# Delta-rule scan: two of the four transfers that spread the masked products are issued by ScalarE in place of SyncE

## The chip, the cores and the metric

The kernel runs on one core of one Trainium2 chip. The metric is the device time of one execution in microseconds (us). A core has five engines that each follow their own list of instructions: TensorE (PE), VectorE (DVE), ScalarE (ACT), GpSimd (POOL) and SyncE (SP). They meet only at semaphores. A transfer (DMA) is issued by an instruction in one engine's list and carried out by the core's 16 DMA engines; its landing adds 16 to a semaphore.

## What is computed

The program is a chain of seven further layers behind a first one; the change lies in the first, a delta-rule attention over 8 sequences of 512 tokens with 16 heads of 16 features. Its heart is a recurrence over the tokens:

```python
def step(M, inp):
    q_t, k_t, v_t, b_t = inp
    out_t = jnp.einsum('bnh,bnhd->bnd', q_t, M)
    retrieved = jnp.einsum('bnhd,bnd->bnh', M, k_t)
    delta = v_t - retrieved
    M = M + b_t[..., None, None] * jnp.einsum('bnh,bnd->bnhd', k_t, delta)
    return (M, out_t)
_, outs = jax.lax.scan(step, M0, xs)
```

The output rows are divided by their root mean square, multiplied by a weight, projected by Wo and added to x. Feed-forward, distance attention, a long convolution, mixtures and a state-space layer follow; the change does not touch them.

## The kernel before

The function `delta_scan` works in 32 chunks of 16 tokens. All 8 sequences and 16 heads of a chunk are treated at once, and one chunk needs the state matrix that the chunk before it left, so the chunks follow each other strictly. Each engine has a body `turn(ch, more)` that is written out for chunk after chunk; the order on an engine is the order in this code, and nothing reorders it. `ch.u` is 0 for the even chunks (0, 2, ...) and 1 for the odd ones: inputs are loaded for two chunks at a time, by the turns of odd chunks. `ch.j` is 0 in the first eight chunks; from the ninth on each turn also projects a finished tile of the output (`tile`, `tile_ready`, `root`, `tile_add`).

What one chunk does, with the lines that matter here:

- PE multiplies the keys with the state (psX, line 3471). DVE subtracts the result from the values (`wg`, L3739) and masks the products of queries and keys that PE formed in the chunk before (`qkm`, L3745, semaphore `qk_done`).
- PE forms the chunk's own key products (psB, L3486); DVE transposes them (`bg`, L3753, `bl_done`) and then solves a triangular system of 16 steps in `solve`: one copy (L3679), then by turns L3698, L3685 and L3692, all on DVE.
- The first reduction of the solve (L3692 with 26 outputs) reads columns of `pb` that ACT copies from `bg` (L3615, and L3617 for a later reduction): DVE waits for `pb_done` there.
- ACT's turn is, in this order: two scaled copies `wtm` (L3609), `take_out` (L3588: it reads what `within` left in PSUM and waits for `o_ps`), the two copies to `pb` (L3615, L3617, both behind `bl_done`), `tile_ready` (L3596, L3597), in odd chunks the load of `vT` (L3562), `keys` (L3579, L3582), `root` (L3602), four loads of `nbg` (L3571) and in odd chunks four loads of `qj` (L3567).
- The masked products lie in `qkm`, in four strips of 32 partitions. Four transfers from SBUF to SBUF, one for each strip, put them on the diagonal of `qkx` (L3386, 32 KB each). They wait for `qk_done` of this chunk and for `o_ps` of the chunk before, since `qkx` is a single buffer. PE reads `qkx` in `within` (L3439), which stands in its list behind the psB products of the next chunk and ahead of the products of L3505; L3505 also waits for `take_out`.
- SP's turn is in odd chunks: four loads of `kj` (L3344), eight of `kx` (L3353), the four `qkx` transfers, four loads of `nbx` (L3360). In even chunks: one load of `ng` (L3356), the four `qkx` transfers, four loads of `qx` (L3348).
- POOL folds the feed-forward weights beside the scan (`Butterfly.run`, L246 and L254), with a 1 MB load of `bf_w` (L228) every 24 us or so.
- `fill` (L3460) puts matmuls on PE whose results nobody reads.

Of the kernel before, what the change touches and what calls it, by code (L numbers as in the profile page):

```python
# [3244 lines left out]
def delta_scan(nc, core, tag, kx, feat, tok_nbk, wo, rms_w, masks, beside):  # L3245
# [17 lines left out]
    with ExitStack() as ctx:  # L3263
        sbf = lambda n, s: core.sbuf(f"{tag}_{n}", s, ctx)
        G, Q, H = 4, 32, 2
# [20 lines left out]
        qkm = sbf("qkm", [P, 2, G, G, CT])  # L3286
        qkx = sbf("qkx", [P, G, G, G, CT])
# [38 lines left out]
        strip = lambda n: slice(n * Q, (n + 1) * Q)  # L3326

        def chunks(eng, body):

            for n in range(CHUNKS):  # L3330
                body(Chunk(n // NCB, n % NCB // 2, n % 2), min(2, CHUNKS - 1 - n))
# [4 lines left out]
        @block.sync  # L3336
        def _(sp):

            flat = lambda rows: rows.rearrange("p j c g t -> p (j c g t)")

            def load_kj(c):
                src = k_d[c].rearrange("(i p) j n -> j p i n", i=G)
                for j in range(G):
                    sp.dma_start(kj[strip(j), j].rearrange("p i c g t -> p i (c g t)"), src[j]).then_inc(kj_in, 16)  # L3344

            def load_qx(c):
                for i in range(G):
                    sp.dma_start(flat(qx[strip(i), i]), q_d[c][strip(i)].rearrange("p j n -> p (j n)")).then_inc(qx_in, 16)  # L3348

            def load_kx(c):  # L3350
                for h in range(2 * G):
                    rows = slice(h * HD, (h + 1) * HD)
                    sp.dma_start(flat(kx[rows, h]), k_d[c][rows].rearrange("p j n -> p (j n)")).then_inc(kx_in, 16)  # L3353

            def load_ng(c):
                sp.dma_start(flat(ng[c % 2]), n_d[c].rearrange("p j n -> p (j n)")).then_inc(ng_in, 16)  # L3356

            def load_nbx(c):
                for j in range(G):
                    sp.dma_start(nbx[strip(j), j].rearrange("p (g f) -> p g f", g=G), nb_rows[c][j]).then_inc(nbx_in, 16)  # L3360

            load_ng(0)
            load_kx(0)
            sp.wait_ge(cleared, 1)
            load_qx(0)
            sp.wait_ge(zeroed, 1)
            load_nbx(0)
            sp.wait_ge(cleared, 2)
            load_kj(0)
            sp.dma_start(wo_sb[:], wo.rearrange("(k p) n -> p k n", p=P)).then_inc(loaded, 16)  # L3370
            sp.dma_start(rw[:], rms_w).then_inc(loaded, 16)

            def turn(ch, more):
                nxt = ch.pair(1)
                if ch.u and more:
                    ch.wait(sp, x_ps, 1, 1)
                    load_kj(nxt)
                    ch.wait(sp, b_ps, 1, 1)
                    load_kx(nxt)
                if ch.u == 0 and more == 2:  # L3380
                    ch.wait(sp, nbm_done, 2, 2)
                    load_ng(nxt)
                ch.wait(sp, qk_done, 1, 1)
                ch.wait(sp, o_ps, 1, 0)
                for g in range(G):
                    sp.dma_start(qkx[strip(g), g].rearrange("p j i t -> p (j i t)"),  # L3386
                                 qkm[strip(g), ch.n % 2].rearrange("p j i t -> p (j i t)")).then_inc(qkx_in, 16)
                if ch.u == 0 and more == 2:
                    ch.wait(sp, q_ps, 1, 2)
                    load_qx(nxt)  # L3390
                if ch.u and more:
                    ch.wait(sp, e_ps, 2, 2)
                    load_nbx(nxt)

            sp.wait_ge(zeroed, 3)
            chunks(sp, turn)
            sp.wait_ge(qkx_in, 64 * CHUNKS)

# [158 lines left out]
        @block.scalar  # L3557
        def _(act):
            a = nc.scalar.activation

            def load_v(c):
                act.dma_start(vT[:].rearrange("p j c g t -> p (j c g t)"), v_d[c].rearrange("p j n -> p (j n)")).then_inc(v_in, 16)  # L3562

            def load_qj(c):
                src = q_d[c].rearrange("(i p) j n -> j p i n", i=G)
                for j in range(G):
                    act.dma_start(qj[strip(j), j].rearrange("p i c g t -> p i (c g t)"), src[j]).then_inc(qj_in, 16)  # L3567

            def load_nbg(c):
                for g in range(G):  # L3570
                    act.dma_start(nbg[strip(g), c % 2, g].rearrange("p i f -> p (i f)"),  # L3571
                                  nb_cols[c][g].unsqueeze(0).broadcast_to([2, CT, 512])).then_inc(nbg_in[c % 2], 16)

            def keys(ch):

                split = lambda t: t.rearrange("p (j g) t -> p j g t", g=G)
                ch.pair_in(act, ng_in, 16)
                ch.wait(act, b_ps, 1, 0)
                a(split(wg[:, :, 1, :]), ng[ch.n // 2 % 2][:, :, ch.u], ACT.Identity).then_inc(wn_done, 1)  # L3579
                ch.wait(act, q_ps, 1, 0)  # L3580
                for e in range(2):
                    a(split(nbm[:, :, e, :]), ng[ch.n // 2 % 2][:, :, ch.u], ACT.Identity, scale=par[:, e:e + 1]).then_inc(nbm_done, 1)  # L3582

            def take_out(ch):

                pos = ch.cc * CT
                ch.wait(act, o_ps, 1, 1)
                a(oTb[:, ch.j % 2, :, pos:pos + CT], psO.rearrange("p j g t -> p (j g) t"),  # L3588
                  ACT.Identity).then_inc(oe_done, 1)

            def tile_ready(y, u, back):

                y.wait(act, y_ps, 1, -back)
                act.wait_ge(oe_done, NCB * (y.j + 1))
                src = oTb[:, y.j % 2, y.cc * KD:(y.cc + 1) * KD, :]
                a(oT[:, u], src, ACT.Identity).then_inc(oT_done, 1)  # L3596
                a(osq[:, u], src, ACT.Square).then_inc(osq_done, 1)  # L3597

            def root(y, u):

                y.wait(act, y_ps, 1, 1)
                a(r[:, u:u + 1], (psY, al)[u][:, D:D + 1], ACT.Sqrt, scale=1.0 / D, bias=eps6[:]).then_inc(root_done, 1)  # L3602

            def turn(ch, more):

                ch.wait(act, wt_done, 1, 1)
                ch.wait(act, w_ps, 1, 0)
                for e in range(2):
                    a(wtm[:, :, e, :], wg[:, :, 0, :], ACT.Identity, scale=par[:, e:e + 1]).then_inc(wtm_done, 1)  # L3609

                if ch.last():
                    take_out(ch.last())

                ch.wait(act, bl_done, 1, 1)
                a(window(pb, 7, [[8, 6], [48, 13]]), window(bg, 3 * Q + 2, [[1, 6], [Q, 13]]),  # L3615
                  ACT.Identity).then_inc(pb_done, 1)
                a(window(pb, 14 * 48 + 15, [[16, 8], [128, 7]]), window(bg, 9 * Q + 8, [[1, 8], [Q, 7]]),  # L3617
                  ACT.Identity).then_inc(pb_done, 1)

                if ch.j:  # L3620
                    tile_ready(Chunk(ch.j - 1, ch.pp, ch.u), 0, 0)

                if more:
                    if ch.u:
                        load_v(ch.pair(1))
                    keys(ch.next())

                if ch.j:
                    root(Chunk(ch.j - 1, ch.pp, ch.u), 0)
                if more:  # L3630
                    ch.wait(act, m_ps, 2, 0)
                    load_nbg(ch.n + 1)
                if more and ch.u:
                    ch.wait(act, o1_ps, 1, 1)
                    load_qj(ch.pair(1))

            load_v(0)
            act.dma_start(par[:], masks[0]).then_inc(masks_in, 16)
            act.dma_start(own[:].rearrange("p a t -> p (a t)"), masks[2]).then_inc(masks_in, 16)
            act.dma_start(causal[:], masks[1]).then_inc(masks_in, 16)  # L3640
            act.wait_ge(masks_in, 48)
            keys(Chunk(0, 0, 0))
            act.wait_ge(zeroed, 2)
            load_nbg(0)
            act.wait_ge(zeroed, 4)
            load_qj(0)
            act.wait_ge(eps_set, 1)
            chunks(act, turn)
            take_out(Chunk(TPB - 1, NCB // 2 - 1, 1))
            for n in range(NCB):  # L3650
                tile_ready(Chunk(TPB - 1, n // 2, n % 2), n % 2, min(n, 1))
                if n:
                    root(Chunk(TPB - 1, (n - 1) // 2, (n - 1) % 2), (n - 1) % 2)
            root(Chunk(TPB - 1, NCB // 2 - 1, 1), 1)
# [230 lines left out]
```

## Time and profile before

| | us |
|---|---|
| median of three runs | 2507.13 (2505.23 to 2515.93) |
| the profiled execution's own time | 2502.61 |
| its span, first to last instruction | 2500.8 |
| of this, the scan's chunks 1 to 31 | from 203.9 to 636.8 |

The profiled execution is one execution of the same program; its own time is a little below the three timed ones. In a timeline row the first number is the start from the beginning of the span, the second the time that the group took; "SPq" and "ACTq" are instructions of an engine's sequencer, here the issues of transfers. A number in square brackets is the time for which the engine was idle ahead of the row, and behind the arrow stands what ended it.

### The profile page before, as it was taken

Reading aid. Unit: us, or ns where it says so; the run is one execution under the profiler, and the core shown is the slowest. Engines: PE = TensorE matmul, PEld = TensorE weight load, DVE = VectorE, ACT = ScalarE, POOL = GpSimd, SP = SyncE. Lnnn points to the kernel's source line nnn. Section 1 sums busy time; section 2 is a strip of 40 time slices with the busy share of each in tenths; the row PEclk is TensorE's granted clock in tenths of the full one; section 3 lists DMA queues with packets and bytes.
Section 4 is the critical chain, followed back from the end, with each engine's and each line's share of the span. In section 5 each row is a group of like instructions: output and inputs, shape, how many; then the busy total and the mean of one; then the engine's idle time right before and its main releaser. Section 6 shows DMA issues by size and latency. Waiting matters only on the chain. (4 is left out here: it accounts for less than half of the span.)

```text
span 2500.8 us, 54327 instructions
## 1 busy us (share of the span) xinstructions
PE 2211.0 (88%) x21028; PEld 1618.1 (65%) x21028; DVE 1817.7 (73%) x4456; ACT 1406.0 (56%) x2163; POOL 1121.3 (45%) x1165
## 2 busy tenths in 40 slices
PE   7966767777899989999999988999898989999979
PEld 4535555555788845565656655998477856666669
DVE  6666778777766687888888865896664757767766
ACT  4531122222333279999999985655212567777755
POOL 4337999995001166677666852000351022233220
PEclk9989999999999989999999999999999999999999
DMA  5555444553100112112112211000001000000002
GB/s 175 152 156 163 128 147 138 166 156 102 63 1 14 41 55 69 56 61 69 57 54 74 67 44 38 1 1 1 15 1 40 1 1 1 1 1 1 1 1 68
DMA packets 158719, 148.87 MB, mean 60 GB/s; under 512 B 21440, under 2 KB 141376, under 8 KB 155392
## 3 DMA queue, kind: packets, MB, share of 16 engines
q1 hardware_dynamic: 138704, 105.51, 14.2%
q0 software_dynamic: 3456, 23.07, 2.8%
q10 hardware_dynamic: 16304, 16.83, 2.3%
q8 instruction: 168, 2.75, 0.5%
q14 instruction: 87, 0.71, 0.1%
HBM read 100.51 MB, written 40.63 MB: 56 GB/s over the span
## 5 line engine op out<-in xcount | busy, mean ns | idle before, releaser
L2057 DVE TENSOR_SCALAR_CACHE_REDUCE a_dist<-a_ring 128x512 f32<-128x512 f32 x512 | 336.5, 686 | 83.9 <-PE a_ring L1629 70.7
L2013 POOL TENSOR_SCALAR a_dist<-a_dist,a_mq 128x512 f32<-128x512 f32 x512 | 350.0, 712 | 66.6 <-ACT a_mq L1948 66.6
L1938 ACT ACTIVATE a_pT<-a_psT 128x1024 f32<-128x1024 f32 x256 | 257.9, 1025 | 56.4 <-PE a_psT L1641 40.1
L1641 PE MATMUL a_psT<-ident,a_dist 128*128 128x128 f32 x2048 | 272.2, 278 | 15.8 <-ACT a_pT L1938 12.6
L1641 PEld LDWEIGHTS a_psT<-ident,a_dist 128*128 128x128 f32 x2048 | 237.1, 143 | 56.7 <-issue 34.8
L1932 ACT ACTIVATE a_dist<-a_dist 128x2048 f32<-128x2048 f32 x128 | 236.0, 1901 | 14.5 <-DVE a_dist L2057 11.3
L3609 ACT ACTIVATE ds_wtm<-ds_wg,ds_par 128x256 f32<-128x256 f32 x64 | 29.1, 502 | 273.0 <-DVE ds_wg L3739 268.9
L1629 PE MATMUL a_ring<-a_stack 102*128 102x512 bf16 x512 | 175.5, 393 | 6.7 <-DVE a_dist L2057 5.1
L1258 POOL TENSOR_TENSOR c_y<-c_prod 128x1024 f32<-128x1024 f32 x16 | 39.2, 2472 | 294.5 <-DVE c_prod L1296 294.5
L1654 PE MATMUL a_psO<-a_pT,a_va 128*32 128x512 f32 x1024 | 133.7, 603 | 5.6 <-ACT a_pT L1938 5.6
L437 ACT ACTIVATE f_h<-a_psT,bf_bias_h 128x512 f32<-128x512 f32 x64 | 44.2, 690 | 125.9 <-PE a_psT L371 125.9
L2670 POOL TENSOR_TENSOR s_xdec<-s_xdt,s_dv 128x512 f32<-128x512 f32 x24 | 25.1, 1044 | 197.9 <-ACT s_dv L2596 188.1
L2696 DVE SCALAR_TENSOR_TENSOR s_xbc<-s_padded,sw_cw,s_xbc 128x512 f32<-128x512 f32 x144 | 107.5, 748 | 6.8 <-ACT s_xbc L2556 3.1
L1629 PEld LDWEIGHTS a_ring<-a_stack 102*128 102x128 bf16 x512 | 45.1, 98 | 101.9 <-DVE a_dist L2057 79.1
L2678 POOL TENSOR_TENSOR s_lt<-s_lt,s_gm 128x1024 f32<-128x1024 f32 x32 | 75.3, 2353 | 76.3 <-ACT s_lt L2606 76.3
L246 POOL TENSOR_TENSOR bf_t<-bf_up,bf_w 128x512 f32<-128x512 f32 x80 | 99.9, 1281 | 9.6 <-DMA bf_w<-in_up_w_dram 8.1
L246 POOL TENSOR_TENSOR bf_t<-bf_down_t,bf_w 128x512 f32<-128x512 f32 x80 | 100.3, 1288 | 1.6
L2405 PE MATMUL s_psP<-s_xnT,sw_win 128*128 128x512 f32 x192 | 91.5, 609 | 9.7 <-ACT s_xnT L2548 6.0
L1991 POOL TENSOR_TENSOR bf_up<-a_raw 128x512 f32<-128x512 f32 x28 | 32.8, 1173 | 145.6 <-DVE a_raw L2069 145.6
L480 DVE TENSOR_TENSOR f_h_lo<-f_h,f_h_hi 128x512 fp32r<-128x512 f32 x128 | 89.8, 702 | 4.4
L437 ACT ACTIVATE f_h<-f_psH,bf_bias_h 128x512 f32<-128x512 f32 x64 | 44.2, 690 | 70.1 <-PE f_psH L371 70.1
L478 DVE CAST f_h_hi<-f_h 128x512 fp32r<-128x512 f32 x128 | 56.1, 438 | 36.3 <-ACT f_h L437 36.1
(467 smaller groups left out, 6315.6 us busy)
## 6 DMA issues: line engine op xcount, KB each, us to landing
a_stack<-a_parts_dram SPq DMA_DIRECT2D x384, 64.0 KB
a_parts_dram<-a_parts SPq DMA_DIRECT2D x32, 384.0 KB, 2.4
bf_w<-in_up_w_dram POOLq DMA_DIRECT2D x10, 1024.0 KB, 5.6
bf_w<-in_down_w_dram POOLq DMA_DIRECT2D x10, 1024.0 KB, 7.7
ds_nbg<-tok_nbk ACTq DMA_DIRECT2D x128, 64.0 KB
feat_v<-di_part SPq DMA_DIRECT2D x16, 256.0 KB, 2.6
tok_nbk<-di_nbk SPq DMA_DIRECT2D x16, 256.0 KB, 2.9
feat_k<-di_part SPq DMA_DIRECT2D x16, 256.0 KB, 3.4
```

The lines of the kernel that those rows point to most:

```text
L246: e.tensor_tensor(t, v[:, :, i % 2, :], w, ALU.mult).then_inc(self.step, 1)
L437: gelu = lambda out: nc.scalar.activation(out, psH[m % 2], ACT.Gelu, bias=self.bf.bias_h[:, m:m + 1])
L480: tt(self.h_lo[:, m, :], self.h[:, n % self.RING, :], self.h_hi[:, m, :], ALU.subtract).then_inc(self.h_lo_done, 1)
L1629: mm(to[:], stack[0:NROW, u, 0, i, q * P:(q + 1) * P], stack[0:NROW, u, 1, i, :], start=True, stop=True).then_inc(ring_in, 1)
L1641: last = turn(psT[:, u % 2, kb, q * P:(q + 1) * P], dist[:, g % 2, i, q, k * P:(k + 1) * P], core.ident[:])
L1654: last = mm(psO[i * PAD:(i + 1) * PAD, :], va[:, par, kb, c:c + PAD], pT[:, i, kb // 2, kb % 2, :], start=(kb == 0), stop=(kb == TPB - 1))
L1932: a(dist[:, g % 2, i], dist[:, g % 2, i], ACT.Sqrt)
L1938: a(pT[:, u // 2, u % 2], psT[:, u % 2], ACT.Exp).then_inc(exp_done, 1)
L2013: last = nc.gpsimd.tensor_scalar(d, d, -1.0, mq[:, g % 2, i, q:q + 1], ALU.mult, ALU.add)
L2057: ts(dist[:, gg % 2, i, q, :], ps[:], 1e-12, 3.0e38, ALU.max, ALU.min, accum_out=mq[:, gg % 2, i, q:q + 1]).then_inc(ring_out, 1)
L2405: last = nc.tensor.matmul(out, lhsT, rhs, start=(k == 0), stop=(k == KD - 1))
L2696: last = stt(o, src[:, j:j + S], cw[:, c, j:j + 1], o, ALU.mult, ALU.add)
```

## The change

SP issues the transfers of strips 0 and 1 as before. Those of strips 2 and 3 are issued by ACT. In ACT's turn they stand behind `take_out` and ahead of the two copies to `pb`, with the same two waits. One wait for the memset of `qkx` is added on ACT ahead of the chunks; it stands behind a wait that already covers it.

```diff
@@ block.sync, turn @@
                 ch.wait(sp, qk_done, 1, 1)
                 ch.wait(sp, o_ps, 1, 0)
-                for g in range(G):
+                for g in range(G // 2):
                     sp.dma_start(qkx[strip(g), g].rearrange("p j i t -> p (j i t)"),
                                  qkm[strip(g), ch.n % 2].rearrange("p j i t -> p (j i t)")).then_inc(qkx_in, 16)
@@ block.scalar, turn @@
                 if ch.last():
                     take_out(ch.last())
 
+                ch.wait(act, qk_done, 1, 1)
+                ch.wait(act, o_ps, 1, 0)
+                for g in range(G // 2, G):
+                    act.dma_start(qkx[strip(g), g].rearrange("p j i t -> p (j i t)"),
+                                  qkm[strip(g), ch.n % 2].rearrange("p j i t -> p (j i t)")).then_inc(qkx_in, 16)
+
                 ch.wait(act, bl_done, 1, 1)
                 a(window(pb, 7, [[8, 6], [48, 13]]), window(bg, 3 * Q + 2, [[1, 6], [Q, 13]]),
                   ACT.Identity).then_inc(pb_done, 1)
@@ block.scalar, ahead of the chunks @@
             act.wait_ge(eps_set, 1)
+            act.wait_ge(zeroed, 3)
             chunks(act, turn)
```

ACT's list in the ninth chunk (the first with a tile), before:

```order
L3609 ACTIVATE ds_wtm<-ds_wg,ds_par 128x16x16 x2
L3588 ACTIVATE ds_oTb<-ds_psD0 128x16x16
L3615 ACTIVATE ds_pb<-ds_bg 128x6x13
L3617 ACTIVATE ds_pb<-ds_bg 128x8x7
L3596 ACTIVATE ds_oTq<-ds_oTb 128x256
L3597 ACTIVATE ds_oTq<-ds_oTb 128x256
```

The same place with the change (L3621 and L3623 are the copies to `pb` that were L3615 and L3617):

```order
L3609 ACTIVATE ds_wtm<-ds_wg,ds_par 128x16x16 x2
L3588 ACTIVATE ds_oTb<-ds_psD0 128x16x16
L3617 DMA ds_qkx<-ds_qkm 32x256 x2
L3621 ACTIVATE ds_pb<-ds_bg 128x6x13
L3623 ACTIVATE ds_pb<-ds_bg 128x8x7
L3596 ACTIVATE ds_oTq<-ds_oTb 128x256
L3597 ACTIVATE ds_oTq<-ds_oTb 128x256
```

Two issues of transfers now stand ahead of everything in ACT's turn but the `wtm` copies and `take_out`. SP's list differs only in the count of the `qkx` row, 2 in place of 4; the lists of PE, DVE and POOL are the same.

## Rows read from the trace of the kernel before

**Rows 1.** The page: busy time of each engine and its share

```profile
PE 2211.0 (88%) x21028; PEld 1618.1 (65%) x21028; DVE 1817.7 (73%) x4456; ACT 1406.0 (56%) x2163; POOL 1121.3 (45%) x1165
```

**Rows 2.** Stretches by window: length, busy of each engine, granted clock, DMA share, GB/s

```profile
core 0: us, PE busy (x) PEld busy (x) DVE busy (x) ACT busy (x) POOL busy (x), PEclk, DMA share, GB/s
203.85:636.80 432.95, 309.35 (x9316) 246.80 (x9316) 334.50 (x1034) 109.04 (x320) 384.16 (x317) 0.97 0.48 137
314.98:328.32 13.34, 9.58 (x302) 7.76 (x302) 10.95 (x35) 3.73 (x11) 12.87 (x11) 1.00 0.63 202
297.89:314.98 17.09, 11.83 (x302) 9.61 (x302) 10.96 (x34) 3.69 (x11) 16.78 (x15) 0.80 0.33 94
522.44:540.00 17.56, 12.25 (x302) 9.47 (x302) 11.04 (x34) 3.74 (x11) 17.00 (x15) 0.81 0.67 174
607.55:623.48 15.93, 12.67 (x302) 10.24 (x302) 11.02 (x35) 3.68 (x11) 0.00 (x0) 0.79 0.16 44
```

**Rows 3.** Last work of POOL's folding and of DVE's scan, by line

```profile
L254 POOL TENSOR_TENSOR bf_down_t<-bf_t x40: 1259/1278/1301, 445.0 to 598.8; 128x512 f32<-128x512 f32 x40
L3718 DVE BATCH_NORM_STATS2 bn<-X x32: 409/418/420, 312.7 to 649.2; 128x6 f32<-128x256 f32 x32
```

**Rows 4.** Timeline of an odd chunk without a late transfer

```profile
314.98 0.42 DVE L3739 TENSOR_TENSOR ds_wg<-ds_vT,ds_psXQ 128x256 f32<-128x256 f32 x1
...
317.05 0.38 ACT L3588 ACTIVATE ds_oTb<-ds_psD 128x256 f32<-128x256 f32 x1 [0.70 <-PE ds_psD L3439]
317.35 0.34 ACT L3615 ACTIVATE ds_pb<-ds_bg 128x78 f32<-128x78 f32 x1
...
318.13 0.24 DVE L3692 TENSOR_REDUCE ds_al<-ds_pb 128x26 f32<-128x78 f32 x1
```

**Rows 5.** Timeline of the next chunk, with a late transfer

```profile
330.74 0.65 PE L3439 MATMUL ds_psD<-ds_qkx,ds_dm 128*32 128x64 f32 x32 [0.87 <-DMA ds_qkx<-ds_qkm]
...
331.46 0.38 ACT L3588 ACTIVATE ds_oTb<-ds_psD 128x256 f32<-128x256 f32 x1 [1.78 <-PE ds_psD L3439]
331.50 1.16 SPq L3386 DMA_DIRECT2D ds_qkx<-ds_qkm  x2
331.74 0.33 ACT L3615 ACTIVATE ds_pb<-ds_bg 128x78 f32<-128x78 f32 x1
...
332.18 0.24 DVE L3692 TENSOR_REDUCE ds_al<-ds_pb 128x26 f32<-128x78 f32 x1 [0.74 <-ACT ds_pb L3615]
```

**Rows 6.** Chain of waits in the scan (184 to 640): us in total, times, longest

```profile
DVE ds_al L3692 <- ACT ds_pb L3615: 11.9, 8, 3.5
...
PE ds_psD L3439 <- DMA ds_qkx<-ds_qkm: 8.1, 6, 3.2
...
PE ds_psD L3439 <- issue: 4.4, 2, 2.2
```

**Rows 7.** Timeline, three of those eight waits of DVE

```profile
304.52 0.24 DVE L3692 TENSOR_REDUCE ds_al<-ds_pb 128x26 f32<-128x78 f32 x1 [3.52 <-ACT ds_pb L3615]
375.19 0.24 DVE L3692 TENSOR_REDUCE ds_al<-ds_pb 128x26 f32<-128x78 f32 x1 [2.02 <-ACT ds_pb L3615]
512.20 0.24 DVE L3692 TENSOR_REDUCE ds_al<-ds_pb 128x26 f32<-128x78 f32 x1 [2.09 <-ACT ds_pb L3615]
```

**Rows 8.** Timeline of SP over the odd chunk of rows 4

```profile
316.67 5.48 SPq L3353 DMA_DIRECT2D ds_kx<-feat_k  x8
322.25 3.47 SPq L3386 DMA_DIRECT2D ds_qkx<-ds_qkm  x4
325.77 3.66 SPq L3360 DMA_DIRECT2D ds_nbx<-tok_nbk  x4
```

**Rows 9.** Timeline of ACT at the scan's start

```profile
183.60 2.06 ACTq L3567 DMA_DIRECT2D ds_qj<-feat_q  x4
185.77 0.91 ACT L3609 ACTIVATE ds_wtm<-ds_wg,ds_par 128x256 f32<-128x256 f32 x2 [4.11 <-issue]
```

**Rows 10.** Issues by line: duration ns min/median/max, first and last start us

```profile
L3386 SPq DMA_DIRECT2D ds_qkx<-ds_qkm x128: 507/592/1689, 187.1 to 627.6; - x128
L3571 ACTq DMA_DIRECT2D ds_nbg<-tok_nbk x128: 597/599/1200, 180.5 to 617.6; - x128
L3562 ACTq DMA_DIRECT2D ds_vT<-feat_v x16: 338/339/381, 173.9 to 596.7; - x16
```

**Rows 11.** Timeline, four issues of nbg by ACT

```profile
334.61 2.51 ACTq L3571 DMA_DIRECT2D ds_nbg<-tok_nbk  x4
```

## The prediction

> **What bounds the kernel now.** The page comes first: PE is busy for 88% of the span, DVE for 73% [rows 1], but that mean covers stages with different limits, and the change lies in one of them. So I read the scan by windows. Its chunks 1 to 31 take 432.95 us, in which DVE is busy for 334.50, PE for 309.35 and ACT for 109.04 [rows 2]. No engine fills the stretch: each chunk is a chain that passes between PE and DVE, and DVE's solve is its longest piece. A chunk without trouble takes 13.34 us, with DVE busy for 10.95 [rows 2]. POOL looks full (384.16 us), but its folding ends 50 us ahead of the scan: its last group starts at 598.8, DVE's last at 649.2 [rows 3]. What lengthens DVE's chain lengthens the kernel, until it is many times what is discussed here.
>
> In the timeline of one clean chunk the reader is to see how close ACT's copy to pb comes to that chain. `take_out` starts at 317.05, the copy L3615 0.30 us behind it at 317.35, and it ends at 317.69. The reduction L3692 that needs it starts at 318.13 [rows 4]. In a chunk where it was late it ran from 331.74 to 332.07 and the reduction began at 332.18, 0.11 later [rows 5]. So in the clean chunk the copy could have been later by 318.13 - 317.69 - 0.11 = 0.33 us. More than that shifts the solve and everything behind it.
>
> Last the waits, for what the change can win. DVE waits for that copy 8 times, 11.9 us in all, and PE waits in `within` for the `qkx` transfers 6 times, 8.1 us [rows 6]. These are mostly the same events: transfers late, `within` late, `take_out` late, and the copy stands behind `take_out` ([rows 5] show one such chain). Two of the eight, 2.02 and 2.09 us [rows 7], go with the two waits of PE of 4.4 us that are put down to issue [rows 6], at which no transfer is named. That leaves 11.9 - 4.1 = 7.8 us that late `qkx` transfers cost. Why they are late: in an odd chunk SP issues eight `kx` loads first (5.48 us), then the four `qkx` transfers in 3.47 us up to 325.72 [rows 8], though nothing but the `kx` issues stood between it and them for those 5.48 us, and PE could not read them before 330.74 [rows 5].
>
> **The change, part by part.** Two issues leave SP. They were the last two of a group of four. SP's share starts when it did and ends a pair earlier; two take 1.16 us in [rows 5], half of 3.47, that is 1.74, in [rows 8]. ACT's pair now goes out right behind `take_out`, in odd chunks some 5 us before SP gets to its own.
>
> Two issues come to ACT. Does ACT stand still while it issues? [rows 9] say so: four `qj` issues run from 183.60 to 185.66, and the `wtm` copy behind them starts at 185.77, after 4.11 us of idle time that no engine caused. It was held by the issues and ran 0.11 us after the last. What does one issue cost there? No row shows `qkx` on ACT. The nearest are the same transfer on SP, 592 ns median, and ACT's `nbg` load, also to 32 partitions, 599 ns median [rows 10]. A pair takes 1.16 us on SP [rows 5] and half of 2.51, 1.25 us, on ACT [rows 11]. I take 1.20. The bounds: 0.34 us each as ACT's `vT` load, 339 ns [rows 10], which with a gap of 0.03 makes 0.71 for the pair; and 1.74 us, half of the 3.47 in [rows 8], where issues were stretched.
>
> Where does the pair begin? SP's first `qkx` issue follows 0.04 us behind the start of `take_out`, both released by the same semaphore [rows 5]; ACT's will too. So the copy to pb starts 0.04 + 1.20 + 0.11 = 1.35 us behind the start of `take_out`, where it was 0.30: it is 1.05 late. 0.33 is free, so the reduction and all that follows shift by 0.72 us. Over 32 chunks: 23.0 us. The first has no `take_out`, but the same two issues ahead of the copy; I count it in full.
>
> What this delay drags along: behind the copy in ACT's list stand the second copy, `tile_ready`, the `vT` load, `keys`, `root` and the loads of `nbg` and `qj`. The second copy is read three reductions further on, and PE waits for `tile_ready` and `keys` only late in the solve, which itself moves by 0.72: nothing. The waits on `qk_done` and `o_ps` on ACT add nothing, as `qkm` is written ahead of `bg` on DVE and `take_out` has waited for `o_ps` already. The wait on the memset is covered.
>
> What comes back: the reduction now waits in every chunk, and lateness of `within` adds on top. A transfer may be later by the SP pair saved (1.20) and by the stretch of the chunk between (0.72), 1.92 us in all, before it is seen. In terms of DVE's wait, a lateness is the wait plus the 0.33 that were free. The longest was 3.52 + 0.33 = 3.85; 1.93 of it remains. The other five are below 1.92 (7.8 - 3.52 = 4.3 us for five, 0.74 in [rows 5]) and vanish. The two waits without a transfer stay, and count 2.02 + 0.33 and 2.09 + 0.33, 4.77 together. Sum of DVE's waits there after the change: 23.0 + 1.9 + 4.8 = 29.7; before: 11.9. The difference is 17.8 us.
>
> The sum is made against the profiled execution's 2502.61: 2520.4. The median of the three runs is 4.5 us above that execution, so the same 17.8 on the median give **2525 us**.
>
> A rule speaks for less: the Trainium skill, page "DMA: Bandwidth & Descriptors", section "Issuing engines are not separate DMA queues", says that starting transfers from several engines saves only the sequencer's time, as all of them interleave on the same 16 engines. If that is all, nothing lands earlier by a less crowded queue; it would leave the late landings as they are. No row here decides it, and it stands behind the first rival.
>
> **The rivals.**
>
> 1. The late transfers stay late. For it: the chunks after them carry much traffic (the DMA share is 0.63 in the odd chunk before [rows 5] [rows 2]), and the last `qkx` issue ended 5 us before PE could go on, longer than the issues themselves. Against: SP's ring then holds two transfers fewer. The sum is 23.0 + 8 x 0.33 = 25.6 us more: 2533. This is what the rule above would make of it.
>
> 2. The issue on ACT is cheap or does not hold ACT: not slower. If each costs what `vT` costs (0.71 the pair), the copy is 0.04 + 0.71 + 0.11 - 0.30 = 0.56 late and DVE shifts by 0.23 a chunk, 7.4 us; the longest lateness keeps 3.85 - 1.20 - 0.23 = 2.4, with the 4.8 that is 7.2, and 7.4 + 7.2 - 11.9 is +2.7: 2510. If the copies went past the issues, no chunk would shift, the waits fall from 11.9 to 4.1 + (3.52 - 1.20) = 6.4, and the time is 2501.6. For it: ACT starts an issue while earlier activations still run. Against: what matters is an activation behind issues, and [rows 9] show that held. It decides where the pair holds ACT for less than 0.04 + x + 0.11 = 0.63, x = 0.48 us: below, no chunk is shifted.
>
> 3. Issues stretched as in [rows 8]: a pair of 1.74 makes 1.26 a chunk, 40.3 + 6.7 - 11.9 = +35: 2542. For it: in odd chunks SP issues `kx` at the same time. Against: ACT's `nbg` issues hold 597 to 599 ns in minimum and median [rows 10].
>
> 4. TensorE's clock. Three windows of a chunk have a granted clock of 0.80, 0.81 and 0.79, and took 17.09, 17.56 and 15.93 us where a chunk at 1.00 took 13.34 [rows 2]; the first had the 3.52 us wait, in which PE stood idle. The last had 1.09 of waiting and lost 1.5 more to the clock (15.93 - 13.34 - 1.09). The change puts 0.7 us of idle time on PE into each chunk, ahead of the tile. If in six more chunks the clock fell to the lower of its two levels (1.2 GHz of 2.4) for part of their time, at 2.6 us each (between 1.5 and 4.2), the time is 2541. Against: clean chunks with gaps keep 1.00.
>
> **How the numbers follow.** Forecast 55% (own range 2517 to 2531: a pair of 1.13 to 1.3, with more or less of the late landings gone); rival 1 12%; rival 2 cheap 8%, not held 8%; rival 3 7%; rival 4 10%. The predicted time is the forecast's, 2525. The range is 2508 to 2541: below it lies the case where ACT is not held and a tail of the cheap one, above it half of rivals 3 and 4. 0.5% is 12.5 us, about what a measurement of this kernel can tell from no change; slower by more begins at 2519.7. That takes in rivals 1, 3 and 4 (29%) and most of the forecast (45 of 55): 0.74. Rival 2 and the forecast's lower end make within 0.5%, 0.22. Faster by more than 12.5 us would need more than all 11.9 us of these waits back, with nothing paid: 0.04.
>
> **What would show it.** ACT's two `qkx` issues, starting 0.04 behind `take_out`, 0.5 to 0.6 us each; the copy to pb 1.35 behind `take_out` in place of 0.30; DVE waiting for it in all 32 chunks, 0.72 each, in sum near 30 us; a clean chunk of 14.06 in place of 13.34; PE's waits for `qkx` down from 8.1 to 2 us or less; the scan's end 18 us later and all stages behind it as long as before. It would be wrong if the copy starts before the issues end, if the issues take 0.3 or 0.9 us, or if the granted clock in the scan leaves 0.97.

## The result

The changed kernel takes 2530.16 us (median of four runs, 2526.04 to 2536.14), the kernel before, run beside it, 2509.85. The ratio is 1.0098, with an interval from 1.0063 to 1.0133: slower by 0.6 to 1.3% (the two medians alone give 1.0081). Timed again later (x4 below) it is 1.0085, from 1.0056 to 1.0114.

The profile after belongs to the slowest of the four runs: span 2534.5 us. What answers to [rows 4], an odd chunk of the changed kernel (timeline):

```profile
321.04 0.38 ACT L3588 ACTIVATE ds_oTb<-ds_psD 128x256 f32<-128x256 f32 x1 [0.71 <-PE ds_psD L3439]
321.10 1.21 ACTq L3617 DMA_DIRECT2D ds_qkx<-ds_qkm  x2
...
322.35 0.35 ACT L3621 ACTIVATE ds_pb<-ds_bg 128x78 f32<-128x78 f32 x1 [0.93 <-issue]
322.80 0.24 DVE L3699 TENSOR_REDUCE ds_al<-ds_pb 128x26 f32<-128x78 f32 x1 [0.72 <-ACT ds_pb L3621]
...
323.75 1.10 PE L3452 MATMUL ds_psY<-ds_wo,ds_oTq 128*128 128x256 f32 x4 [1.09 <-DVE ds_pb L3692]
```

ACT issues its pair in 1.21 us, and the copy to pb (L3621 now) starts 322.35 - 321.04 = 1.31 us behind `take_out`; it was 0.30. DVE waits 0.72 us for it. In the even chunk behind it SP issues its own `qkx` pair at the same moment, and ACT's pair takes longer:

```profile
335.06 0.38 ACT L3588 ACTIVATE ds_oTb<-ds_psD 128x256 f32<-128x256 f32 x1 [0.70 <-PE ds_psD L3439]
335.10 1.16 SPq L3386 DMA_DIRECT2D ds_qkx<-ds_qkm  x2
335.12 1.42 ACTq L3617 DMA_DIRECT2D ds_qkx<-ds_qkm  x2
336.59 0.34 ACT L3621 ACTIVATE ds_pb<-ds_bg 128x78 f32<-128x78 f32 x1 [1.15 <-issue]
337.03 0.24 DVE L3699 TENSOR_REDUCE ds_al<-ds_pb 128x26 f32<-128x78 f32 x1 [0.92 <-DVE ds_pb L3692]
```

The last row names DVE's own product as what ended the wait, but an instruction just ahead on the same engine ends when the idle time begins; the row above shows the copy that the reduction waited for (it ends at 336.93, 0.10 ahead). All issues of `qkx` on ACT, duration in ns min/median/max:

```profile
L3617 ACTq DMA_DIRECT2D ds_qkx<-ds_qkm x64: 562/605/1753, 183.8 to 642.9; - x64
```

The chain of waits of the scan in the changed kernel, which answers to [rows 6] (us in total, times, longest):

```profile
DVE ds_al L3699 <- ACT ds_pb L3621: 22.9, 23, 2.3
...
DVE ds_al L3699 <- DVE ds_pb L3692: 7.7, 9, 0.9
```

```profile
PE ds_psY L3452 <- DVE ds_pb L3692: 30.0, 23, 2.2
...
PE ds_psD L3439 <- DMA ds_qkx<-ds_qkm: 0.9, 1, 0.9
```

DVE waits in all 32 chunks, 22.9 + 7.7 = 30.6 us, where it was 11.9. PE's wait for `qkx` is down from 8.1 us to 0.9. And PE waits 30.0 us ahead of the tile (L3452), 1.09 in the odd chunk above, where the kernel before has 4.6 us in 15 waits: DVE does not wait for PE there, but TensorE stands idle.

Windows over chunks 1 to 30, first of the kernel before, then of the changed one with an odd and an even chunk (columns as in [rows 2]):

```profile
203.85:623.48 419.63, 300.42 (x9046) 239.43 (x9046) 324.28 (x1002) 105.65 (x309) 384.16 (x317) 0.97 0.49 141
```

```profile
202.90:640.18 437.28, 306.41 (x9046) 247.89 (x9046) 324.03 (x1001) 108.39 (x309) 382.27 (x315) 0.95 0.47 135
318.97:332.99 14.02, 9.55 (x302) 7.76 (x302) 10.94 (x35) 3.81 (x11) 13.79 (x12) 1.00 0.47 144
332.99:347.21 14.22, 9.55 (x302) 7.76 (x302) 10.93 (x35) 3.79 (x11) 13.67 (x13) 1.00 0.44 146
```

Each engine does the work that it did; the chunks are 14.02 and 14.22 us long in place of 13.34, and their granted clock is 1.00 all the same. The 0.95 is a mean: chunk by chunk, 11 of the 30 have 0.79 to 0.89 and the others 1.00; in the kernel before it is 4 of 30. DVE's last group of the scan answers to [rows 3]:

```profile
L3725 DVE BATCH_NORM_STATS2 bn<-X x32: 407/417/419, 316.7 to 668.1; 128x6 f32<-128x256 f32 x32
```

The scan ends 668.1 - 649.2 = 18.9 us later. From there to the end this profile has 2534.5 - 668.1 = 1866.4 us, the one before 1851.6; that part of 14.8 us comes back below.

### The profile page after: what moved, and what is told of

It reads as the page before. It is cut to its first block and busy times, and to the rows that moved or that the text cites. A ratio compares the mean times of both kernels' runs of the same rounds, so it can differ in the third digit from the quotient of the medians.

```text
span 2534.5 us, 54358 instructions
## 1 busy us (share of the span) xinstructions
PE 2230.5 (88%) x21028; PEld 1636.4 (65%) x21028; DVE 1817.7 (72%) x4456; ACT 1407.7 (56%) x2163; POOL 1119.4 (44%) x1165
## 5 line engine op out<-in xcount | busy, mean ns | idle before, releaser
L3460 PE MATMUL ds_psXQ<-ident 128*128 128x256 f32 x240 | 71.4, 438 | 15.5 <-DVE ds_pb L3692 8.5
L3699 DVE TENSOR_REDUCE ds_al<-ds_pb 128x26 f32<-128x78 f32 (+6 forms) x224 | 57.6, 257 | 37.2 <-ACT ds_pb L3621 22.9
```

## The experiments

Each ran beside the kernel before on the same chip; x, y and z ran on three different ones. All ratios are to the kernel before, and 0.1% is 2.5 us. "+" and "-" lines are against the changed kernel unless said otherwise.

**x1: the pair behind the copies.** ACT copies to pb first, then issues.

```diff
-                (ACT's two waits and two qkx transfers)
                 ch.wait(act, bl_done, 1, 1)
                 a(window(pb, 7, ...), ...).then_inc(pb_done, 1)
                 a(window(pb, 14 * 48 + 15, ...), ...).then_inc(pb_done, 1)
+                (ACT's two waits and two qkx transfers)
```

> The changed kernel, but ACT issues its two transfers behind the two copies to pb instead of ahead of them. If the loss comes from ACT being held ahead of the copies, DVE no longer waits for them: clean chunks are back at 13.34 us, the waits of DVE for pb fall from 30.6 us to below 5 us, and since late qkx landings stay away as well it is 8 to 12 us below the kernel before (ratio 0.995 to 0.997). If splitting the group over two queues is itself what costs (transfers in each other's way, or the granted clock), it stays 10 us or more above the kernel before.

Measured: 0.9991 (0.9969 to 1.0013). The loss of the change is gone, which speaks for the hold and against the split as its cause. But the gain was not there either: I had 0.995 to 0.997. DVE's waits for the copy are 4.8 us, as expected; the time went elsewhere. The profile is that of the slowest of x1's twelve executions, 2517.8 us where the median is 2501.7. The timeline of one of its chunks:

```profile
403.87 0.35 ACT L3615 ACTIVATE ds_pb<-ds_bg 128x78 f32<-128x78 f32 x1
403.94 0.56 ACTq L3623 DMA_DIRECT2D ds_qkx<-ds_qkm  x1
...
404.53 0.61 ACTq L3623 DMA_DIRECT2D ds_qkx<-ds_qkm  x1
405.24 0.42 ACT L3596 ACTIVATE ds_oTq<-ds_oTb 128x256 f32<-128x256 f32 x1 [0.82 <-issue]
405.57 0.40 ACT L3597 ACTIVATE ds_oTq<-ds_oTb 128x256 f32<-128x256 f32 x1
...
406.22 1.10 PE L3452 MATMUL ds_psY<-ds_wo,ds_oTq 128*128 128x256 f32 x4 [1.03 <-DVE ds_al L3705]
```

The hold has only moved on. Now it delays `tile_ready` (L3596, L3597), and PE stands idle ahead of the tile for 1.03 us. The row names DVE, but PE starts 0.25 us behind the end of L3597 in nearly every chunk of x1, whatever DVE does. In the kernel before, L3597 ended 0.50 us ahead of the tile, so by an estimate from the two only 0.25 us were free, and PE stands idle for 0.33 us:

```profile
319.00 1.13 PE L3452 MATMUL ds_psY<-ds_wo,ds_oTq 128*128 128x256 f32 x4 [0.33 <-DVE ds_pb L3685]
```

Over chunks 1 to 30 the granted clock is 0.94, where the kernel before has 0.97:

```profile
201.66:629.80 428.14, 309.31 (x9046) 248.59 (x9046) 325.24 (x1002) 109.30 (x309) 382.56 (x315) 0.94 0.48 138
```

That is not yet the loss. The chunk shown took 13.33 us at a clock of 1.00, like most of those with a gap of about 1.03. The time went into six chunks of 16.3 to 17.9 us, five of them at 0.71 to 0.81, in which other things come together: `kx` 3.7 us late in one, a second ACT issue of 1.45 us and a gap of 1.86 in one, and in four a stop of PE of 1.2 to 2.9 us for which the profile names no cause. Such stops are in the kernel before too (three, 1.6 to 2.2 us). And over all twelve executions x1's clock averages 0.970, no lower than the kernel before beside it. So x1 shows that the tile's inputs have little room; how much of the missing gain the gap cost through the clock it does not show.

**x2: the hold without the transfers' move.** Against the kernel before: SP issues all four as ever; ACT also issues two of the same size to a tile that nobody reads. DVE waits for them too before it writes `qkm` again, two chunks later (not shown).

```diff
+                ch.wait(act, spare_in, 32, 0)
+                ch.wait(act, qk_done, 1, 1)
+                ch.wait(act, o_ps, 1, 0)
+                for g in range(G // 2, G):
+                    act.dma_start(spare[strip(g)], qkm[strip(g), ch.n % 2]...).then_inc(spare_in, 16)
                 ch.wait(act, bl_done, 1, 1)
```

> The kernel before, with SP's four qkx transfers as they were, and in addition two transfers of the same size by ACT at the changed kernel's place, from qkm to a scratch tile that nobody reads (each chunk also waits for the pair of the chunk before, long landed). This has the hold on ACT without the earlier landing. If the hold is the whole cost: DVE waits for pb in all 32 chunks, 0.72 us in odd and 0.92 in even ones, and the late landings remain and show on top (waits of 35 to 42 us in all): 25 to 32 us above the kernel before, 5 to 8 more than the changed kernel. If the hold is not what costs, it is within 5 us of the kernel before.

Measured: 1.0128 (1.0097 to 1.0160), that is +32 us. Its chain of waits:

```profile
DVE ds_al L3702 <- ACT ds_pb L3624: 34.3, 25, 4.4
...
DVE ds_al L3702 <- DVE ds_pb L3695: 3.7, 4, 0.9
DVE ds_al L3702 <- issue: 3.7, 2, 2.6
```

```profile
PE ds_psD L3441 <- DMA ds_qkx<-ds_qkm: 9.0, 5, 3.3
```

41.7 us of waits, and PE still waits 9.0 us for `qkx`. So the hold alone costs 41.7 - 11.9 = 29.8 us of waits, and what the changed kernel gets back from `qkx` landing earlier is 41.7 - 30.6 = 11.1 us; I had expected 5 to 8. These are differences between single profiles, and x2 moves two transfers more in each chunk. Its granted clock over chunks 1 to 30 is 0.92, so not all of the +32 us are waits.

**x3: SP's order.** Against the kernel before, ACT untouched: in odd chunks the four `qkx` transfers stand ahead of the eight `kx` loads.

```diff
+                (waits, then the four qkx transfers)
                 if ch.u and more:
                     ch.wait(sp, b_ps, 1, 1)
                     load_kx(nxt)
-                (waits, then the four qkx transfers)
```

> The kernel before, ACT untouched, but in odd chunks SP issues its four qkx transfers ahead of the eight kx loads. If qkx landed late because it stood behind kx on SP, PE's waits for qkx fall from 8.1 us to below 1 us and the time by 6 to 9 us (ratio 0.996 to 0.998), unless kx now comes late, which would show as waits of PE for kx at the psB products. If the landings were late because of the traffic on the DMA engines, whoever issues and in whatever order, the waits stay near 8 us and the time is the same.

Measured: 1.0113 (1.0087 to 1.0138), the wrong way. No wait of PE for `qkx` is left, but this has come:

```profile
PE ds_psB L3487 <- DMA ds_kx<-feat_k: 38.0, 12, 5.6
```

SP issues the `kx` loads behind four more issues, some 3 us later, and they landed too late for 12 of the 15 chunks that read them first, by up to 5.6 us: how late a landing comes is not the shift of its issue. The expectation named this wait as a way out, not as the likely case. It settles against this order, and leaves open how much of the lateness of `qkx` in the kernel before is the queue ahead of it and how much the traffic: PE's products with `kx` stand ahead of `within`, so while they wait, a late `qkx` does not show.

**x4: the changed kernel once more.**

> The changed kernel once more, on the same chip as the three others. The scan's waits give +18 to +21 us; the first measurement said 1.0098 (24.6 us) with an interval of 0.35% to either side, and its profile showed 12 us more outside the scan. If those belong to the run and not to the change, this gives 1.007 to 1.009 and stages behind the scan as long as in the kernel before to within 3 us.

Measured: 1.0085 (1.0056 to 1.0114). Its chunks 1 to 30 take 437.99 us, 18.4 more than in the kernel before (17.7 in the profile after). Its scan ends at 675.1 of 2529.6 us, 25.9 later than in the kernel before, but 5.8 of these had gone by when chunk 1 began. The end at 675.1 leaves 1854.5 behind it, near the 1851.6 of the kernel before. Over all profiles here, whose kernels are alike behind the scan, that stretch lies between 1851.6 and 1866.4 us. So most of the 14.8 us outside the scan in the profile after belong to that execution; x4 shows 2.9.

**y1: the pair behind `keys`,** ahead of `root`.

```diff
                 if more:
                     if ch.u:
                         load_v(ch.pair(1))
                     keys(ch.next())
+                (ACT's two waits and two qkx transfers)
                 if ch.j:
                     root(Chunk(ch.j - 1, ch.pp, ch.u), 0)
```

> The changed kernel, but ACT's two transfers stand behind tile_ready and keys, ahead of root. In x1 they stood ahead of tile_ready; the tile's inputs came later, PE stood idle ahead of the tile and the granted clock was at its lower level for 48 us of the scan against 24 before. If that is where x1 lost its gain, here PE's wait ahead of the tile is back at 0.3 us, DVE's waits for pb stay below 6 us, the low clock at 20 to 30 us, and the time is 6 to 12 us below the kernel before (0.995 to 0.998). If the late kx loads and the traffic took it, it is within 3 us of the kernel before, like x1.

Measured: 0.9962 (0.9947 to 0.9977), some 9.5 us below the kernel before. DVE's waits for the copy are 5.2 us, 6.7 less than before, and `kx` is late by 3.8 us in two chunks, nearly as in x1 (4.8). So late `kx` loads are not what sets x1 apart. The nine executions lie between 2492.4 and 2501.9 us at clocks of 0.971 to 0.974; x1's twelve reach from 2493.6 at 0.974 to 2517.8 at 0.964. The two intervals touch, and the two ran on different chips. An even chunk:

```profile
330.23 0.35 ACT L3615 ACTIVATE ds_pb<-ds_bg 128x78 f32<-128x78 f32 x1
...
330.56 0.57 ACTq L3631 DMA_DIRECT2D ds_qkx<-ds_qkm  x1
330.67 0.40 ACT L3596 ACTIVATE ds_oTq<-ds_oTb 128x256 f32<-128x256 f32 x1
...
331.16 0.62 ACTq L3631 DMA_DIRECT2D ds_qkx<-ds_qkm  x1
331.29 0.41 ACT L3579 ACTIVATE ds_wg<-ds_oTq 128x256 f32<-128x256 f32 x1
331.59 0.90 ACT L3582 ACTIVATE ds_nbm<-ds_oTq,ds_par 128x256 f32<-128x256 f32 x2
...
331.89 1.13 PE L3452 MATMUL ds_psY<-ds_wo,ds_oTq 128*128 128x256 f32 x4 [0.33 <-DVE ds_pb L3692]
```

The issues stand behind L3596, L3597, L3579 and L3582 in the list, and yet the first starts before any of these and the second ahead of L3579 and L3582. So ACT goes on to an issue while activations ahead of it have not begun. Issues there hide beside five activations, and PE's gap is back at 0.33 us.

**y2: one transfer on ACT**, three on SP, at the changed kernel's place.

```diff
-                for g in range(G // 2):        # SP
+                for g in range(3):
-                for g in range(G // 2, G):     # ACT
+                for g in range(3, G):
```

> The changed kernel with one transfer on ACT (strip 3) and three on SP. One issue of 0.56 us ends 0.7 us behind the start of take_out and the copy starts 0.8 behind it, against 0.63 that costs nothing: DVE waits 0.1 to 0.2 us a chunk for pb in place of 0.72 to 0.92, 3 to 6 us in all, plus what late landings are left. Theory of the hold: 0 to +5 us against the kernel before. If instead the split over two queues costs by itself, it is near the changed kernel, +15 us or more.

Measured: 1.0010 (0.9990 to 1.0030). In an odd chunk the copy starts 0.68 us behind `take_out` and DVE is held up by less than 0.1:

```profile
315.70 0.38 ACT L3588 ACTIVATE ds_oTb<-ds_psD 128x256 f32<-128x256 f32 x1 [0.70 <-PE ds_psD L3439]
315.77 0.56 ACTq L3617 DMA_DIRECT2D ds_qkx<-ds_qkm  x1
316.38 0.35 ACT L3621 ACTIVATE ds_pb<-ds_bg 128x78 f32<-128x78 f32 x1 [0.29 <-issue]
316.83 0.24 DVE L3699 TENSOR_REDUCE ds_al<-ds_pb 128x26 f32<-128x78 f32 x1
```

Over the scan DVE waits 7.2 us for the copy, in 7 chunks. This profile is that of the fastest of twelve executions (2497.8 us, the median is 2508.1).

**y3: all four on ACT**, none on SP (SP's waits and loop are removed, ACT's runs over `range(G)`).

> All four transfers on ACT, none on SP. If the cost is the time for which issues hold ACT ahead of the copies, it goes up by 0.65 us with each further issue: copy 2.6 to 2.9 us behind the start of take_out, DVE waits 1.9 to 2.2 us in each chunk, 60 to 70 us in all, and the kernel is 55 to 80 us above the kernel before, with some more low clock. If ACT took in issues without being held, it would be near the changed kernel.

Measured: 1.0374 (1.0347 to 1.0402), +94 us. Chain of waits up to 680 us (the scan ends at 741) and window of chunks 1 to 30:

```profile
DVE ds_al L3694 <- ACT ds_pb L3616: 64.6, 28, 3.1
```

```profile
PE ds_psY L3447 <- DVE ds_pb L3687: 56.2, 21, 3.4
```

```profile
204.90:712.19 507.29, 363.80 (x9046) 296.11 (x9046) 326.50 (x1001) 108.26 (x309) 381.19 (x315) 0.81 0.39 116
```

The wait is close to what the hold said: up to the scan's end 71.1 us in 31 chunks, 2.3 each, a little above my 60 to 70. The total is further above my 55 to 80, and the clock goes with it: 0.81, with 27 of the 30 chunks at 0.79 to 0.81. Thirty chunks of 13.34 are 400.2 us; 507.3 - 400.2 - 67.4 of waits in these chunks leaves about 40 us, by this estimate the price of TensorE at the lower of its two levels, 1.2 GHz, for part of nearly every chunk. Its gap ahead of the tile was 2.7 us on the mean (63.8 in 24 up to the scan's end).

**y4: matmuls in the new gap.** The changed kernel, and PE runs two matmuls without a reader ahead of the tile.

```diff
+                ch.wait(pe, qk_done, 1, 1)
+                fill(2)
                 ch.wait(pe, sol, PER, 4 + 6)
```

> The changed kernel, and PE runs two matmuls that nobody reads while it stands idle ahead of the tile (0.8 us of the 1.05 us that it is idle there). DVE's waits stay at 27 to 31 us. If part of the changed kernel's loss is the granted clock (at its lower level for 41 to 44 us of the scan, 24 before), the low clock falls to 24 us or less and the time by 2 to 6 us against the changed kernel, to 1.006 to 1.008. If the clock plays no part there, it equals the changed kernel, 1.0085.

Measured: 1.0054 (1.0034 to 1.0074), somewhat below what I had, against 1.0085 and 1.0098 for the changed kernel, whose intervals overlap with this one. DVE's waits for the copy are 26.6 us in 32 chunks, just below my 27 to 31, and the clock over chunks 1 to 30 is up from 0.95:

```profile
202.57:632.85 430.28, 324.02 (x9166) 256.05 (x9166) 323.80 (x1002) 108.55 (x309) 382.00 (x315) 0.99 0.47 137
```

Three of the 30 chunks are below a clock of 1.00 in place of 11 (9 in x4's profile). So in these profiles the clock stays up where the gap is filled. In time it is less clear: of the 7.0 us by which these chunks are shorter than in the profile after, 3.7 are shorter waits for the copy.

**z1 and z2: one such matmul in y1 and in the kernel before.** The edit is that of y4 with `fill(1)`.

> y1 (ACT's two transfers behind keys) and one matmul that nobody reads ahead of PE's tile, as the version that might beat all others. PE stands idle there for 0.33 us in y1, so one matmul of 0.4 us fits. If low clock still costs y1 something (24 us of its scan), this is 0.993 to 0.996 against the kernel before; if the clock in y1 falls only after landings that come late, which this matmul does not fill, it equals y1, 0.996.

> The kernel before with the same one matmul. y4 took 0.3% off the changed kernel by filling PE's idle time ahead of the tile. If that was the low clock that the change itself had brought in (by 0.7 us more of idle time there), the kernel before has little of it to win: 0.998 to 1.001. If the matmuls win the same 0.3% here, the low clock was there before the change, and y4 says nothing of the change.

Measured: z1 0.9947 (0.9925 to 0.9968), z2 0.9984 (0.9956 to 1.0011). z1 has the lowest ratio, some 13 us below the kernel before; whether it is faster than y1 its interval doesn't tell, so which of my two cases for it holds stays open. z2 lies where I put it, but its interval holds both 0.3% and nothing, so it does not settle how much of y4's gain is low clock that the change brought in.

## Why the prediction was right, point by point

The forecast was 17.8 us more on the median, 2525, in a range of 2508 to 2541. Measured were 2530.16 us, 20.3 more between the medians, and by the ratios 24.6 and 21.3 us; the scan in the profile gave 18.9. The mechanism was the one forecast; that the sum of the waits came so close is in part luck, as the second point shows.

- **ACT is held by its issues.** Right. The copy started 1.31 us behind `take_out` (1.35 forecast) and DVE waited 0.72 us (0.72) in the odd chunks. One, two and four issues give less than 0.1, 0.72 and, on the mean, 2.3 us, and x1 and y1, with the issues behind the copies, none. Rival 2, cheap or free issues, is out: an issue of `qkx` on ACT takes 0.605 us in the median and 0.562 at the least.
- **The size of the pair.** 1.20 us was right in odd chunks (1.21), low in even ones, where SP issues its `qkx` pair at the same moment: 1.42 here, and 0.92 us of waiting. This is a part of rival 3, which I had put down for odd chunks and the `kx` loads. Single issues were stretched to 1.75 us. The sum of DVE's waits came out right even so (29.7 forecast, 30.6 measured), because two errors cancel. Sixteen chunks at 0.72 and sixteen at 0.92 make 26.2, more than my 23.0; the other 4.4 are chunks where ACT's pair was stretched further, up to 2.35 us, and one late landing. Against that less came late than I had left in: PE's wait for `qkx` was 0.9 us, I had kept 1.9, and the two waits without a transfer did not recur. In the kernel before, PE had already run 31 and 23 of the 32 matmuls of `within` when it stopped, so these were no late `qkx` but stops without a named cause; x4 has one of 2.9 us elsewhere. That none lengthened DVE's waits for the copy in the profile after is luck.
- **What comes back.** Right: 8.1 us of PE's waits went to 0.9. x2 isolates it: with the same hold and SP's four transfers as before, PE waits 9.0 us for `qkx` and DVE 11.1 us more for the copy. Nor does the longer chunk only hide it: in x1, y1 and z1, whose usual chunk is as short as before, PE waits 1.0, 1.8 and 1.3 us for `qkx`, and in z2, with all four on SP, 11.6. Rival 1 is out. The rule that I had set beside it (the Trainium skill, page "DMA: Bandwidth & Descriptors", section "Issuing engines are not separate DMA queues": a second issuing engine saves the sequencer's time and no more) is not refuted by this: what was saved is a sequencer's time, ACT's pair going out at 321.10 in the chunk shown, ahead of SP's first `kx` load at 322.79, rather than behind the last. It is not small here, though; it was worth 11 us of waits.
- **The clock.** Rival 4 had 10%, and part of it came true beside the forecast: 0.95 over chunks 1 to 30, from 0.97. In us it is little in the scan: 437.28 - 400.2 leaves 37.1 above clean chunks, some 29 of them the waits, 8 the rest; before, 19.4 with 11.9 of waits, 7.5 the rest. x4's profile had 37.8 with 27.2 of waits. By this estimate 0.5 to 3 us are the clock's; y3 shows what it becomes with a larger gap, about 40. Over whole executions its share is open. x4's six average 0.966, the kernel before beside them 0.970, and executions of one kernel differ with the clock: the kernel before beside z took 2497.6 us at 0.974 and 2523.7 at 0.965. No run here separates what the clock costs from what lowers it.
- **The stages behind the scan** were to be as long as before. They were 14.8 us longer in the profile after and 2.9 in x4's; most of that is how executions differ, not the change.

What I had not seen is that the free 0.33 us behind `take_out` was not the only tight place: x1 showed that the tile's inputs have as little room. And y4 showed that PE's idle time there goes with a lower clock though DVE does not wait for PE; what that costs in time is not shown apart from the rest.

## What to carry to other kernels

Issuing one of these 32-partition transfers costs the issuing engine's list about 0.6 us (the `vT` load on ACT 0.34). So ask of the engine that takes it over what stands behind the issue in its list and when that is read; the engine's low busy share (ACT was at 25% in the scan) says nothing about it. Put issues behind the activations that others wait for, where an issue can start while these are still to begin: the same two transfers gave +0.9% ahead of a 0.3 us copy and -0.4% behind it and the activations up to `keys`. And a load moved 3 us back in a queue can land more than 5 us late.

## What the hardware showed beyond that

- An issue on ACT starts while activations ahead of it in the list have not begun (y1: issue at 330.56, L3596 ahead of it in the list at 330.67), but an activation behind it waits for its end (x1: 0.82 us of idle time put down to issue).
- A `qkx` pair took longer on ACT when SP issued its own `qkx` pair at the same time: 1.42 us in the usual even chunk, against 1.21 in the usual odd one, where SP is at the `kj` and `kx` loads.
- TensorE's granted clock was below 1.00 in more chunks where it stood idle longer at a stretch, whether or not another engine waited. Such chunks, out of 30: 4 in the kernel before (its gap ahead of the tile 0.33 us), 5 in y1 (0.33), 11 and 9 in the changed kernel (1.09 and 1.29), 29 in y3 (2.7), and 3 in y4 with the gap filled. The tile's gap is not the whole of it: x3 has 11 with a gap of 0.33, and PE waiting up to 5.6 us for `kx`.
